# Later pacing of 32 small scatters, and their read-back moved behind the fifth expert's weights

## The chip, the cores and the metric

The kernel runs on one core of a Trainium2 chip. The time is device microseconds (us) of one whole execution. Three timed executions of the kernel before took 656.32, 656.92 and 656.56 us; the median is 656.56 us.

## The reference, cut to what matters

The program has two layers over x of shape (2, 1024, 128). Layer 0 is causal attention times the SiLU of a mixture of experts. Layer 1 is a rotation memory (cumulative sums of x times cosine and sine of a phase, a norm, two matrices with GELU) times the SiLU of a second mixture of experts. The change touches only the second mixture:

```python
expert_inputs = einsum('GSEC,GSM->EGCM', dispatch, x)        # 8 experts, 8 groups, 64 slots
layer_w0 = einsum('EGCM,EMH->EGCH', expert_inputs, w0_kernel)
layer_w1 = einsum('EGCM,EMH->EGCH', expert_inputs, w1_kernel)
hidden = gelu(layer_w0, approximate=True) * layer_w1          # H = 688
expert_outputs = einsum('EGCH,EHM->EGCM', hidden, wo_kernel)
out = einsum('EGCM,GSEC->GSM', expert_outputs, combine)       # each token: two of the slots
```

Each of the 2048 tokens goes to two experts. `posn[:, a, n]` holds, for the 128 tokens of tile n, the slot of choice a. A slot's result has to come back to its token.

## The kernel before, in words

Every engine has one program, written out in order, and engines meet only at counting semaphores: `then_inc` raises one, `wait_ge(Z[name], n)` holds the engine until it is n. The sync engine (SP) issues nearly all plain loads, one after another. If one of them waits, all later ones of SP wait behind it. GpSimd (POOL) issues the scatters, also strictly in order.

The second mixture is a loop over 8 experts, numbered 0 to 7. For an expert, TensorE (PE) makes six pairs of products of 512 slots: gate (L1757; L1755 for the last piece, which is gate and up in one) and up (L1760). ScalarE (ACT) applies GELU to each gate product (L733), and VectorE (DVE) multiplies it with the up product (L1362). That multiplication is the "up product" of the title: it raises `hid1_done`, six times for each expert, 48 times in all. After the first two pieces of the next expert, PE does the down product (L1771, 48 matmuls) and raises `ew_free`; DVE copies the result out (L1369) and raises `y1_done`. Behind the last expert PE goes on with the two matrices of the rotation memory's branch (L1815, L1826). Between these multiplications DVE works through the rotation memory, at fixed places in the same loop, and ACT does its sine and absolute value after piece 1 of expert 2 and its cosine after piece 1 of expert 3. The distance from one L1771 to the next is one expert period.

PE may run two pieces ahead. A gate product waits for the GELU of two pieces before (`act1_done`), an up product for the multiplication of two pieces before (`hid1_done`).

The scatters of the change are made by `scatter_destinations` (L553). It writes, for each of the 2 x 16 tiles, 128 words of 4 bytes into the array `dest1` in device memory: at the slot's place, the row that the slot's result must go to. I number them 0 to 31 (16 a + n). SP reads `dest1` back as `dest` (L519) once all 32 have landed. Only then can POOL start the 32 result scatters (L585, four for each expert), which write each expert's output rows to device memory. They go through a buffer of four experts: DVE's copy for expert e waits, from e = 4 on, for the four result scatters of expert e - 4.

`load_expert(e)` on SP (L505 to L513) loads an expert's weights into the buffer that expert e - 2 has left. Its first three loads wait until PE has made the last gate product of expert e - 2, its last three wait for the down product of expert e - 2. In the kernel before, the order on SP is: expert 3's weights, the read-back (L519), expert 4's weights.

Of the kernel before, what the change touches and what calls it, by code (L numbers as in the profile page):

```python
# [18 lines left out]
NT = T // P  # L19
# [190 lines left out]
def build(nc, x, WQ, WK, WV, WO, gate, w1, w2, w3, WomT, b_om, log_scale, gamma, beta, W1T, b1, W2T, b2,  # L210
# [10 lines left out]
    with ExitStack() as ctx:  # L221
# [3 lines left out]
        def sem(name):  # L225
            return ctx.enter_context(nc.semaphore(name))
# [120 lines left out]
        Z = {n: sem(n) for n in names.split()}  # L347
# [34 lines left out]
        def _(sp):  # L382
# [118 lines left out]
            def load_expert(e):  # L501
                s = e % 2
                if e >= 2:
                    sp.wait_ge(Z["g1_ps"], HT * (e - 1))
                sp.dma_start(ew[s][0], w0k[e, :, :]).then_inc(w_in[s], 16)  # L505
                sp.dma_start(ew[s][1][:, TW:H1], w1k[e, :, 0:H1 - TW]).then_inc(w_in[s], 16)
                sp.dma_start(ew[s][1][:, 0:TW], w1k[e, :, H1 - TW:H1]).then_inc(w_in[s], 16)
                if e >= 2:
                    sp.wait_ge(Z["ew_free"], e - 1)
                sp.dma_start(ew[s][2][0:125, 0:4, :],  # L510
                             wok[e, 0:500, :].rearrange("(k p) m -> p k m", p=125)).then_inc(wo_in[s], 16)
                sp.dma_start(ew[s][2][0:124, 4, :], wok[e, 500:H1 - TW, :]).then_inc(wo_in[s], 16)
                sp.dma_start(ew[s][2][P - TW:P, 5, :], wok[e, H1 - TW:H1, :]).then_inc(wo_in[s], 16)  # L513

            for e in range(E):
                load_expert(e)
                if e == 3:
                    sp.wait_ge(Z["scattered"], 16 * 4 * NT)
                    sp.dma_start(dest, dest1[0:SLOTS1, :].rearrange("(p j) o -> p (j o)", p=P)).then_inc(Z["dest_in"], 16)  # L519
            for s in range(4):  # L520
# [11 lines left out]
        @block.gpsimd  # L532
        def _(pool):
            pool.memset(V, 1.0).then_inc(Z["v_ones"], 1)
            pool.memset(mpart[:, :, :], -BIG).then_inc(Z["mem_set"], 1)
            pool.memset(MP, 0.0).then_inc(Z["mem_set"], 1)

            def scatter_rows():

                for a in range(2):  # L540
                    for n in range(NT):
                        pool.wait_ge(Z["e_ready"], SCATTER_AT + SCATTER_EVERY * (NT * a + n))
                        pool.indirect_dma_start(xs0, bass.IndirectOffsetOnAxis(ap=posn[:, a, n:n + 1], axis=0),  # L543
                                                rows[a][:, n, :], None).then_inc(Z["scattered"], 16)

            def scatter_destinations():

                for a in range(2):
                    pool.wait_ge(Z["routed"], 2 + a)
                    for n in range(NT):  # L550
                        if NT * a + n >= 4:
                            pool.wait_ge(Z["hid1_done"], (2 * (NT * a + n) - 4) // 3)
                        pool.indirect_dma_start(dest1, bass.IndirectOffsetOnAxis(ap=posn[:, a, n:n + 1], axis=0),  # L553
                                                idt[:, NT * a + n:NT * a + n + 1], None).then_inc(Z["scattered"], 16)

            pool.wait_ge(Z["pads_in"], 16)
            pool.wait_ge(Z["routed"], 1)
            pool.wait_ge(Z["rows_ready"], 1)
            scatter_rows()

            def scatter_results(c, j):
                pool.wait_ge(Z["y_done"], j + 1)
                pool.nop(nofuse=True)
                pool.indirect_dma_start(ys[0], bass.IndirectOffsetOnAxis(ap=yb0[:, c, ID_META:ROW].bitcast(I32), axis=0),  # L564
                                        yb0[:, c, 0:D], None).then_inc(yb_out[c], 16)
            with pool.Fori(0, NB0 // YB0) as i:
                for c in range(YB0):
                    scatter_results(c, YB0 * i + c)
            for j in range(NB0 // YB0 * YB0, NB0):
                scatter_results(j % YB0, j)  # L570

            pool.wait_ge(Z["pads1_in"], 32)
            pool.wait_ge(Z["pv_done"], NG * NS)
            for s in range(2):
                pool.memset(ew[s][2][0:P - TW, 5, :], 0.0)
            pool.wait_ge(Z["disp_ps"], G1)
            for s in range(2):
                ins = pool.memset(hT1[0:P - TW, s, 5, :], 0.0)
            ins.then_inc(Z["tail_zero"], 1)
            scatter_destinations()  # L580
            pool.wait_ge(Z["dest_in"], 16)
            for e in range(E):
                pool.wait_ge(Z["y1_done"], e + 1)
                for m in range(4):
                    pool.indirect_dma_start(  # L585
                        ys[1], bass.IndirectOffsetOnAxis(ap=dest[:, 4 * e + m:4 * e + m + 1], axis=0),
                        yb1[:, e % 4, m, :], None).then_inc(y1_out[e % 4], 16)
# [3 lines left out]
        def _(act):  # L591
# [91 lines left out]
            for k in range(NG + 1):  # L683
                for step in PLANS[k]:
                    if step[0] == "exp":
                        _, stage, heads = step
                        half, kt = STAGES[stage]
                        r, n = NS * k + stage, 512 - max(0, P * kt - 512 * half)
                        act.wait_ge(Z["e_ready"], e + 1)
                        if r >= 4:  # L690
                            act.wait_ge(Z["pv_done"], r - 3)
                        act.activation(Pr[:, r % 4, heads[0]:heads[-1] + 1, 0:n],  # L692
                                       ring_e[e % 3][:, 0:len(heads) * n].rearrange("p (j c) -> p j c", j=len(heads)), ACT.Exp,
                                       scale=SCALE).then_inc(Z["e_free"], 1)
                        e += 1
                    elif step[0] == "counts":
                        act.wait_ge(Z["gates_d"], 1)
                        act.activation(rs[:, 3, :], rs[:, 2, :], ACT.Exp).then_inc(Z["gates_exp"], 1)
                    elif step[0] == "evac":
                        _, g, half = step  # L700
                        act.wait_ge(Z["pv_done"], NS * g + (NS if half else QT // 2))
                        if g >= 1:
                            act.wait_ge(Z["turned"], 2 * (g - 1) + half + 1)
                        act.copy(OT[:, 512 * half:512 * half + 512], O).then_inc(Z["o_evac"], 1)
                    elif step[0] == "experts0":
                        experts0()
                    elif step[0] == "gate":
                        gate_half(0, step[1])
                    elif step[0] == "scale":
                        act.wait_ge(Z["ld_vecs"], 16 * 5)  # L710
                        act.activation(vecs[:, 12:13], vecs[:, 1:2], ACT.Exp).then_inc(Z["el_done"], 1)
# [63 lines left out]
        def _(dve):  # L775
# [296 lines left out]
            for k in range(-1, NG + 1):  # L1072
                for step in PLANS[k]:
                    if step[0] == "p1":
                        _, g, heads, i, half = step
                        n = min(512, (i + 1) * P - 512 * half)
                        ps = unit_ready()
# [831 lines left out]
```

## Time and profile before

| what | value |
|---|---|
| median of the timed executions | 656.56 us |
| the profiled execution's own time | 658.66 us |
| its span | 656.9 us |
| PE busy / DVE busy / ACT busy / POOL busy | 91% / 75% / 50% / 25% |
| second mixture's experts | about 475 to 613 us of the span |
| packets of the software queue (POOL) | 4320, 3.2% of 16 DMA engines' time |

A timeline row gives start, busy time, engine, line and operation, and in square brackets how long the engine had been idle before it and whose work ended that idle time. "Remote" there means that the awaited semaphore rose just before the start, while no instruction ended at that moment that could have raised it. A row of a windows view gives a stretch, its length, and for each engine the busy time and the number of instructions in it, then the granted share of TensorE's full clock (1.00 is 2.4 GHz, 0.50 is 1.2 GHz), the share of DMA engine time, and GB/s.

### The profile page before, as it was taken

How to read it: one execution, taken by the hardware profiler on the slowest of the kernel's cores; microseconds unless marked ns; L12 is line 12 of the kernel's file. 1: busy time of each engine (PE TensorE's matmuls, PEld its weight loads, DVE VectorE, ACT ScalarE, POOL GpSimd, SP SyncE). 2: the span in 40 equal slices, each digit the busy share in tenths (PEclk: the TensorE clock that was granted, in tenths of full speed). 3: DMA queues.
4: the chain of work that ended last, by engine and by line, in shares of the span. 5: the costliest groups of instructions: out<-in, count | busy, mean ns of one | idle time of the engine just before them, and what ended most of it. 6: DMA issues, size and time to landing. Idle time of an engine off the chain costs nothing. (4 is left out here: it accounts for less than half of the span.)

```text
span 656.9 us, 12382 instructions
## 1 busy us (share of the span) xinstructions
PE 594.7 (91%) x4214; PEld 365.6 (56%) x4215; DVE 490.1 (75%) x1169; ACT 325.3 (50%) x581; POOL 163.5 (25%) x146
## 2 busy tenths in 40 slices
PE   1878999999999999899999998949989799999996
PEld 0523644444453545899999843426446355555654
DVE  7799889999988898455555598246898288987455
ACT  1752367575766766555555467721323352254134
POOL 2000000000143441133333300000068668843200
PEclk9877799999999999999999999987999899999999
DMA  8980606060713181211111070061012114320232
GB/s 191 239 281 22 219 16 185 19 201 3 204 38 100 36 224 25 49 49 45 48 48 40 25 197 2 2 197 61 1 44 66 22 47 120 109 81 17 69 76 64
DMA packets 53692, 57.18 MB, mean 87 GB/s; under 512 B 8651, under 2 KB 37355, under 8 KB 53595
## 3 DMA queue, kind: packets, MB, share of 16 engines
q1 hardware_dynamic: 49310, 49.73, 27.1%
q0 software_dynamic: 4320, 6.81, 3.2%
q8 instruction: 29, 0.48, 0.3%
q14 instruction: 21, 0.16, 0.1%
q10 hardware_dynamic: 12, 0.01, 0.0%
HBM read 42.19 MB, written 18.85 MB: 93 GB/s over the span
## 5 line engine op out<-in xcount | busy, mean ns | idle before, releaser
L692 ACT ACTIVATE arena<-banks 128x512 f32<-128x512 f32 (+1 forms) x304 | 156.2, 586 | 100.3 <-PE banks L1588 57.9
L1602 PE MATMUL banks<-arena 96*128 96x512 bf16 (+3 forms) x384 | 120.4, 343 | 5.2 <-DVE mpart L1082 2.8
L1585 PE MATMUL banks<-arena 128*128 128x512 bf16 (+3 forms) x384 | 116.8, 331 | 6.5 <-ACT arena L692 2.8
L1085 DVE TENSOR_REDUCE mpart<-banks 128x1 f32<-128x512 f32 x128 | 85.8, 684 | 9.0 <-PE banks L1602 8.4
L1082 DVE CUSTOM_DVE_ANT_0 banks<-banks,arena 128x512 f32<-128x512 f32 (+1 forms) x128 | 78.9, 636 | 9.6 <-PE banks L1602 6.6
L1523 PE MATMUL banks<-arena 128*128 128x128 f32 x624 | 76.3, 275 | 1.0 <-ACT arena L642 1.0
L1523 PEld LDWEIGHTS banks<-arena 128*128 128x128 f32 x624 | 72.8, 192 | 1.5 <-ACT arena L642 1.5
L1644 PE MATMUL banks<-arena 128*9 128x512 f32 (+3 forms) x768 | 70.8, 487 | 0.0
L733 ACT ACTIVATE arena<-banks 125x512 f32<-125x512 f32 (+2 forms) x48 | 28.5, 595 | 81.0 <-PE banks L1757 57.0
L1585 PEld LDWEIGHTS banks<-arena 128*128 128x128 bf16 x384 | 38.0, 100 | 53.9 <-issue 26.0
L543 POOL DMA_INDIRECT slots<-rows_a,posn x16 | 15.5, 967 | 194.6 <-PE banks L1585 185.0
L564 POOL DMA_INDIRECT results<-arena x39 | 37.8, 969 | 87.6 <-DVE arena L1016 87.6
L1602 PEld LDWEIGHTS banks<-arena 96*128 96x128 bf16 x384 | 38.2, 101 | 36.3 <-DVE mpart L1082 9.1
L585 POOL DMA_INDIRECT results<-arena x32 | 44.7, 1395 | 37.3 <-DVE arena L1369 24.6
L1006 DVE TENSOR_TENSOR arena<-banks,arena 128x512 f32<-128x512 f32 x39 | 27.0, 692 | 33.9 <-PE banks L1523 29.3
L1588 PE MATMUL banks<-bc 128*128 128x128 bf16 x256 | 49.8, 222 | 0.0
L553 POOL DMA_INDIRECT dest<-idt,posn x32 | 44.8, 1400 | 17.2 <-issue 8.8
L1771 PEld LDWEIGHTS banks<-arena 125*128 125x128 f32 (+2 forms) x384 | 44.1, 191 | 5.2 <-issue 5.2
L1757 PE MATMUL banks<-arena 128*125 128x512 f32 (+1 forms) x80 | 42.1, 608 | 4.9 <-issue 3.4
L1760 PE MATMUL banks<-arena 128*125 128x512 f32 (+1 forms) x80 | 42.7, 616 | 3.9 <-DVE arena L1362 3.4
L1362 DVE TENSOR_TENSOR arena<-banks,arena 125x512 f32<-125x512 f32 (+2 forms) x48 | 32.3, 690 | 18.3 <-PE banks L1760 10.1
L1771 PE MATMUL banks<-arena 125*128 125x128 f32 (+2 forms) x384 | 44.3, 275 | 1.0 <-issue 1.0
(289 smaller groups left out, 901.9 us busy)
## 6 DMA issues: line engine op xcount, KB each, us to landing
k_parts<-arena SPq DMA_DIRECT2D x6, 768.0 KB, 7.8
arena<-in_L_ffn_experts_w_dram SPq DMA_DIRECT2D x2, 2048.0 KB, 10.6
arena<-results SPq DMA_DIRECT2D x8, 512.0 KB, 6.8
arena<-k_parts SPq DMA_DIRECT2D x7, 576.0 KB
arena<-q_parts SPq DMA_DIRECT2D x28, 144.0 KB
arena<-in_L_ffn_w_kernel_dram SPq DMA_DIRECT2D x8, 344.0 KB
slots<-in_pad_rows_dram SPq DMA_DIRECT2D x1, 2535.0 KB, 11.0
arena<-slots SPq DMA_DIRECT2D x39, 65.0 KB
```

The costliest lines, as they stand in the source:

```text
L553: pool.indirect_dma_start(dest1, bass.IndirectOffsetOnAxis(ap=posn[:, a, n:n + 1], axis=0), idt[:, NT * a + n:NT * a + n + 1], None).then_ ...
L585: pool.indirect_dma_start(ys[1], bass.IndirectOffsetOnAxis(ap=dest[:, 4 * e + m:4 * e + m + 1], axis=0), yb1[:, e % 4, m, :], None).then_i ...
L692: act.activation(Pr[:, r % 4, heads[0]:heads[-1] + 1, 0:n], ring_e[e % 3][:, 0:len(heads) * n].rearrange("p (j c) -> p j c", j=len(heads)) ...
L1082: ins = dve.tensor_tensor_reduce(ps[:, 0:n], ps[:, 0:n], tail_mask[:, 512 - n:512], 1.0, -BIG, ALU.add, ALU.max, part)
L1085: ins = dve.tensor_reduce(part, ps[:, 0:n], AX_X, ALU.max)
L1523: ins = pe.matmul(psE[:, c % 2, 512 * w + P * k:512 * w + P * k + P], w_now[:, c % 2, w, P * k:P * k + P], xT0[:, c % 2, :], start=True, s ...
L1585: ins = pe.matmul(ring_e[e % 3][:, at * n:at * n + n], QK[:, slot, j, 1, P * kt:P * kt + P], QK[:, slot, j, 0, q:q + n], start=True, stop= ...
L1588: ins = pe.matmul(ring_e[e % 3][:, at * n:at * n + P], upper_b, ident_b, start=False, stop=True)
L1602: ins = pe.matmul(ps[:, at * n:at * n + n], QK[0:TALL, slot, j, 0, P * i:P * i + P], QK[0:TALL, slot, j, 1, 512 * half:512 * half + n], st ...
L1644: ins = pe.matmul(O[32 * j:32 * j + DK + 1, q:512], V[:, QT * b + kt, HG * hq + j, :], Pr[:, r % 4, j, 0:512 - q], start=(kt == 0), stop=( ...
L1760: pe.matmul(psE[0:hn, k % 2, 512:1024], ew[s][1][:, TW + h0:TW + h0 + hn], XT1[:, e, :, :], start=True, stop=True).then_inc(Z["u1_ps"], 1)
L1771: ins = pe.matmul(psM[:, e % 2, P * m:P * m + P], hT1[HD[k], s, k, P * m:P * m + P], ew[s][2][HD[k], k, :], start=(k == 0), stop=(k == HT ...
```

## The change

Before, scatters 0 to 3 wait for nothing but the routing result, and scatter k from 4 on waits until `hid1_done` is (2k - 4) // 3, so the last waits for 19 (the first piece of expert 3). Now every scatter waits, scatter k for 1 + 3k // 4, so the last waits for 24 (the last piece of expert 3). And the read-back stands on SP behind expert 4's weights, not ahead of them.

```diff
             for e in range(E):
                 load_expert(e)
-                if e == 3:
+                if e == 4:
                     sp.wait_ge(Z["scattered"], 16 * 4 * NT)
                     sp.dma_start(dest, dest1[0:SLOTS1, :].rearrange("(p j) o -> p (j o)", p=P)).then_inc(Z["dest_in"], 16)
...
                 for a in range(2):
                     pool.wait_ge(Z["routed"], 2 + a)
                     for n in range(NT):
-                        if NT * a + n >= 4:
-                            pool.wait_ge(Z["hid1_done"], (2 * (NT * a + n) - 4) // 3)
+                        pool.wait_ge(Z["hid1_done"], 1 + 3 * (NT * a + n) // 4)
                         pool.indirect_dma_start(dest1, bass.IndirectOffsetOnAxis(ap=posn[:, a, n:n + 1], axis=0),
                                                 idt[:, NT * a + n:NT * a + n + 1], None).then_inc(Z["scattered"], 16)
```

What stands on SP between the weights of expert 3 and those of expert 5 (a minus is a row of before alone, a plus one of the changed kernel alone):

```order
 L512 DMA arena<-in_L_ffn_wo_kernel_dram 124x128
 L513 DMA arena<-in_L_ffn_wo_kernel_dram 64x128
-L519 DMA arena<-dest 128x32 [waits scattered]
 L505 DMA arena<-in_L_ffn_w_kernel_dram 128x688 [waits g1_ps]
 L506 DMA arena<-in_L_ffn_w_kernel_dram 128x624
@@ -152,4 +151,5 @@
 L512 DMA arena<-in_L_ffn_wo_kernel_dram 124x128
 L513 DMA arena<-in_L_ffn_wo_kernel_dram 64x128
+L519 DMA arena<-dest 128x32 [waits scattered]
 L505 DMA arena<-in_L_ffn_w_kernel_dram 128x688 [waits g1_ps]
 L506 DMA arena<-in_L_ffn_w_kernel_dram 128x624
```

One load, with its wait, has moved past the six loads of one expert. On POOL, the scatters of the destinations before (L553), and the first result scatters behind them:

```order
L553 DMA dest<-idt,posn 8192x1 [waits routed]
L553 DMA dest<-idt,posn 8192x1 x3
L553 DMA dest<-idt,posn 8192x1 [waits hid1_done] x12
L553 DMA dest<-idt,posn 8192x1 [waits hid1_done,routed]
L553 DMA dest<-idt,posn 8192x1 [waits hid1_done] x15
L585 DMA results<-arena 8192x128 [waits y1_done,dest_in]
```

and now, where the same scatters are L552 and the results L584, since the file is one line shorter:

```order
L552 DMA dest<-idt,posn 8192x1 [waits hid1_done,routed]
L552 DMA dest<-idt,posn 8192x1 [waits hid1_done] x15
L552 DMA dest<-idt,posn 8192x1 [waits hid1_done,routed]
L552 DMA dest<-idt,posn 8192x1 [waits hid1_done] x15
L584 DMA results<-arena 8192x128 [waits y1_done,dest_in]
```

The number and order of POOL's instructions are the same; four of them have a wait that they had not, and all waits are for other counts. The programs of PE, DVE and ACT are unchanged.

## Rows read from the trace of the kernel before

**Rows 1.** Windows view: expert periods, from one L1771 to the next; columns as described above.
```profile
490.80:506.20 15.40, 15.05 (x71) 9.40 (x70) 13.88 (x14) 3.57 (x6) 12.96 (x9) 1.00 0.27 68
506.20:529.70 23.50, 18.61 (x71) 9.85 (x70) 9.79 (x12) 9.87 (x12) 16.19 (x15) 0.85 0.08 17
529.70:545.90 16.20, 15.12 (x72) 9.43 (x71) 14.28 (x13) 8.13 (x9) 10.45 (x7) 1.00 0.38 104
545.90:561.20 15.30, 15.09 (x72) 9.42 (x71) 13.01 (x11) 3.57 (x6) 12.56 (x10) 1.00 0.38 123
```

**Rows 2.** Timeline of PE, 506 to 620 us.
```profile
506.27 5.52 PE L1771 MATMUL banks<-arena 125*128 125x128 f32 x48
...
511.63 1.02 PE L1757 MATMUL banks<-arena 128*125 128x512 f32 x2
...
513.35 1.02 PE L1757 MATMUL banks<-arena 128*125 128x512 f32 x2
...
518.63 1.12 PE L1757 MATMUL banks<-arena 128*124 128x512 f32 x2 [3.41 <-issue]
...
542.35 1.12 PE L1757 MATMUL banks<-arena 128*125 128x512 f32 x2 [1.08 <-DMA arena<-in_L_ffn_w_kernel_dram]
...
613.38 7.03 PE L1815 MATMUL banks<-arena 128*128 128x512 f32 x16
```

**Rows 3.** Timeline of all engines, 506 to 542 us: DVE, ACT and SP.
```profile
506.88 1.28 DVE L1362 TENSOR_TENSOR arena<-banks,arena 125x512 f32<-125x512 f32 x2
...
515.86 0.28 SPq L510 DMA_DIRECT2D arena<-in_L_ffn_wo_kernel_dram  x1
515.86 0.69 DVE L1369 COPY arena<-banks 128x512 f32<-128x512 f32 x1 [7.70 <-remote]
...
517.98 0.60 ACT L733 ACTIVATE arena<-banks 125x512 f32<-125x512 f32 x1 [5.45 <-remote]
...
522.40 1.34 ACT L733 ACTIVATE arena<-banks 125x512 f32<-125x512 f32 x2 [3.83 <-remote]
...
523.16 0.69 DVE L1362 TENSOR_TENSOR arena<-banks,arena 125x512 f32<-125x512 f32 x1 [3.01 <-PE banks L1760]
...
541.71 1.42 DVE L1362 TENSOR_TENSOR arena<-banks,arena 124x512 f32<-124x512 f32 x2
```

**Rows 4.** Timeline of POOL, 479 to 584 us.
```profile
479.22 0.97 POOL L553 DMA_INDIRECT dest<-idt,posn  x1 [4.68 <-DVE posn L1254]
...
505.94 0.96 POOL L553 DMA_INDIRECT dest<-idt,posn  x1 [0.30 <-issue]
...
518.57 0.96 POOL L553 DMA_INDIRECT dest<-idt,posn  x1 [0.30 <-issue]
520.43 0.96 POOL L553 DMA_INDIRECT dest<-idt,posn  x1 [0.91 <-issue]
524.13 2.75 POOL L553 DMA_INDIRECT dest<-idt,posn  x1 [2.75 <-DVE arena L1362]
...
534.42 2.09 POOL L553 DMA_INDIRECT dest<-idt,posn  x1 [0.30 <-issue]
540.73 1.78 POOL L585 DMA_INDIRECT results<-arena  x1 [4.22 <-DMA arena<-dest]
...
584.02 0.96 POOL L585 DMA_INDIRECT results<-arena  x1 [5.89 <-DVE arena L1369]
```

**Rows 5.** Timeline of SP, 486 to 538 us.
```profile
486.67 0.36 SPq L505 DMA_DIRECT2D arena<-in_L_ffn_w_kernel_dram  x1
...
502.42 0.35 SPq L505 DMA_DIRECT2D arena<-in_L_ffn_w_kernel_dram  x1
...
537.69 0.35 SPq L519 DMA_DIRECT2D arena<-dest  x1
538.08 0.43 SPq L505 DMA_DIRECT2D arena<-in_L_ffn_w_kernel_dram  x1
```

**Rows 6.** Windows view, one stretch of 2 us, same columns as Rows 1.
```profile
522.00:524.00 2.00, 0.98 (x2) 0.50 (x2) 0.84 (x2) 1.19 (x2) 0.00 (x0) 0.50 0.03 4
```

## The prediction, made before the changed kernel was run

> **What bounds the kernel now.** I read the page first: PE is busy 91% of the span. Behind the experts its matrices (L1815) start with no wait in front [rows 2], so what the experts save reaches the end. Time is to be had only where PE stands still or is slowed. Then I cut the windows view at the down products, one row for each expert period, and that view decides the case. Three of the four periods shown take 15.3 to 16.2 us; the one from expert 1's down product to expert 2's takes 23.50 [rows 1]. PE did the same work in it (71 instructions, as in its neighbour), but DVE was busy only 9.79 us of it, and the granted clock was 0.85 in the mean, in one stretch of it 0.50, that is 1.2 GHz [rows 1, 6].
>
> The timelines of that period show what happened. PE's down product began at 506.27 and ended 5.52 us later, at 511.79 [rows 2]. Two programs wait for just that: DVE's copy (L1369) and SP's load (L510). Both started at 515.86, so the semaphore was seen some 4.1 us after the work that raises it. PE's next gate product began at 511.63 and ended by 512.65; ACT's GELU of it started at 517.98, 5.3 us late, and ends an idle time that the trace calls remote. ACT's next one, at 522.40, belongs to the gate product that PE began at 513.35, so it was some 8 us late [rows 2, 3]. PE itself then had nothing to do: its next gate product waits for the GELU of two pieces before, and came at 518.63, after 3.41 us with no product at all [rows 2]. After 523.16 everything runs on time again. I call this the hold. It is no lack of an engine: the news of finished PE work came late.
>
> **What the hold goes with.** The scatters. POOL issued 32 of them from 479.22 to 534.42. Twelve stand between 505.94 and 520.43, the last gap aside one every 1.26 us (0.96 busy and 0.30 between), with no wait that held them, because POOL was behind its pacing: at 506.88 DVE made up products 13 and 14, and those allow scatters up to number 24 at once [rows 3, 4]. The first late signal (511.79) comes 5.9 us into this burst, the worst near its end. Then scatter 26 had to wait for up product 16, which itself came late, at 523.16, and in this pause the late signals all arrived [rows 3, 4]. DMA engines were no bottleneck: over the whole period their share is 0.08 [rows 1]. My reading is that a dense run of these 128-word scatters to device memory backs up a path on which PE's signals travel too. The trace shows the coincidence, not the path.
>
> **Term 1, the pacing.** Scatter k now waits for up product 1 + 3k // 4. Up products 13 and 14 of the trace ended by 508.16 [rows 3]; they now release scatters 16 to 18, where before they released all to 24. So the burst ends with 18, at about 510.2 (scatters 16, 17 and 18 at 507.7, 508.9 and 510.2 with 1.26 us each). Scatter 19 waits for up product 15. Without the hold, gate and up of piece 2 end by 513.5 (gate begun at 511.63, the next gate at 513.35 [rows 2]), and DVE's 0.69 us behind them ends by about 514.3. That is a pause of 4 us on POOL just where the hold began. And the pacing now regulates itself: a late up product stops the scatters at once, where before POOL had ten in hand.
>
> What is the period worth without the hold? Its PE work is that of its neighbours. Those took 15.40 and 15.30, and 16.20 with a weight wait of 1.08 inside, so 15.12 [rows 1, 2]. ACT has sine and absolute value here, but is through with them by 512.53 (5.45 before 517.98 [rows 3]), when the gate product it needs has only just ended. I take 15.6, a little above the neighbours, for the two long ACT instructions. Saved: 23.5 - 15.6 = 7.9 us. The low clock falls inside the hold (PE had stood still before it) and goes with it; it is in the 7.9 and not added.
>
> Bounds of this term. Best case: the period sinks to 15.1, 8.4 saved. Worst of this reading: scatters still come in pairs and threes and leave some of the hold. The neighbour 490.8 to 506.2 had scatters in it (9 POOL instructions) and took 15.40 [rows 1], so that density costs next to nothing; I leave 0.5 us for it, and keep 0 to 8 as its bounds.
>
> **Term 2, the read-back on SP.** Before, SP stood at L519 until scatter 31 (issued 534.42) had landed, and went on at 537.69; only then could expert 4's weights be issued, at 538.08, though their buffer had been free since expert 2's last gate product. PE waited 1.08 us for them before 542.35 [rows 2, 5]. Now they are issued when that gate product is done, which without the hold is about 518, 4.3 us or so before they are in (538.08 to 542.35), against a need at about 533. The wait of 1.08 goes. What is late next there is the DVE chain of the period (14.28 busy of 16.20 [rows 1]), so I credit 0.8 and keep 0 to 1.1.
>
> What the move costs: the read-back now stands behind six loads, the last three of which wait for expert 2's down product, about 527 without the hold. Scatter 31 waits for up product 24. Before that was the second of the pair at 541.71, ended 543.1 [rows 3]; minus 7.9 and 0.8 it is 534.5. The scatter starts there and, as before, 3.3 us pass to the read-back (534.42 to 537.69), so L519 is issued at about 538 and the result scatters start at about 541, as before (540.73 [rows 4]). Expert 5's weights, queued behind it, come at 538.4 and are needed at about 547 (expert 4's were at 541, minus 8.7, plus a period of 15.3). DVE's copy for expert 4 (its down product begins at 561.20 [rows 1] and takes 5.5, minus 8.7: 558) needs the first four result scatters, landed by about 549: 9 us to spare. POOL has caught up with the experts before 584.02, where it waited 5.89 us for DVE [rows 4]; 9 us earlier experts leave it just in time. So the move costs nothing; this cover fails only if the read-back comes over 9 us later.
>
> The four scatters that had no wait start at 481 instead of 479.22; nobody waits for them. 32 waits on POOL are met by an engine that is 25% busy.
>
> **Sum.** 7.9 - 0.5 + 0.8 = 8.2 us. The profiled execution took 658.66 us, 2.1 above the median of the three timed ones and with a span of 656.9. The timed ones lie within 0.6 us of each other, so the hold is hardly a rare accident: I take it off the median too, 656.56 - 8.2 = 648.4.
>
> **A rule that speaks against it.** The rows show ACT idle 5.45 us behind a finished PE product while POOL's scatters run [rows 3, 4]. The Trainium skill's page "SBUF — State Buffer", section "Who interferes with whom", says that DMA never contends with a compute engine and that "PE and ACT never wait on anyone". By that rule the scatters could not be what holds PE and ACT. The trace has no case that decides it: the rule is about ports of the on-chip memory, and what came late here is a signal. The rival that follows is worked out from the rows.
>
> **Rivals.**
> (a) The hold has another cause and stays. For it: PE, ACT and DVE share nothing with POOL in the program at that point, and scatters 14 to 18 may still come 1.3 us apart. Against it: it starts in the burst and ends in POOL's pause. Then term 1 is 0, and term 2 alone is left, 0.8 to 1.1 us: about 655.6. The later pacing costs nothing even then: up product 24 ends at 542, the read-back at about 545.5 is still in time.
> (b) The hold shrinks but stays: POOL keeps three or four scatters in hand at 504 to 510, and half of the delay remains. 656.6 - 4 - 0.8 = 652.
> (c) Slower: the hold comes from scatters beside weight loads, and now there are two. Before it, expert 3's weights were issued at 502.42 among scatters [rows 5]. Now expert 4's weights go out near 518 to 526 among scatters 22 to 26, which before they could not, since SP stood at L519 until the scatters had landed. If both periods have a hold of 7.9 us, the time is 656.6 + 7.9 - 1 = 663.5. It decides from the point where expert 3's period exceeds 17 us. Against it: expert 2's weights, issued at 486.67 amid scatters [rows 5], brought no hold.
>
> **Chances.** Forecast, hold gone or nearly: 0.47 (647 to 650). (b): 0.16. (a): 0.20. (c), with smaller second holds that end just above the old time: 0.17. A change under 0.2%, 1.3 us, can't be told from none: faster 0.63, same 0.20, slower 0.17. The range reaches from 647.0 over (b) and (a) to 658.5, and leaves out the bulk of (c); the forecast's own is 647 to 650.
>
> **What would show it.** Right: the period between the down products of experts 1 and 2 at 15.3 to 16, DVE's copy L1368 within 0.2 us of the down product's end, no clock below 1.00 from 475 to 610, no wait of PE for weights at expert 4, POOL in pauses of 2 us and more around 511 to 514, result scatters from about 541. Wrong: a period over 18 us anywhere; then look whether scatters or weight loads surround it. Wrong in term 2: a DVE copy that waits for result scatters.

## The result and the profile after

The changed kernel took 650.28 us (median of 7 executions, 649.79 to 654.0), against a median of 656.92 for the kernel before, measured beside it. The ratio of the two is estimated as 0.9906, with a 95% interval of 0.9879 to 0.9933: 6.2 us faster, 4.4 to 7.9 (the two medians lie 6.6 apart). Forecast were 8.2 us and 648.4.

The profiled execution has a span of 648.0 us against 656.9, 8.9 less. Not all of this is the change: PE's first down product of the experts begins at 489.11 instead of 490.86, so 1.75 us were already won where nothing was changed. Other runs below spread as much there. What the change did stands in the expert periods. The windows view after, cut at the down products (columns as in [rows 1]):

```profile
489.10:504.50 15.40, 15.05 (x71) 9.39 (x70) 13.89 (x15) 3.60 (x7) 12.96 (x9) 1.00 0.26 69
504.50:521.70 17.20, 15.36 (x72) 9.32 (x71) 9.45 (x12) 9.78 (x11) 11.48 (x11) 1.00 0.25 44
521.70:537.10 15.40, 15.07 (x72) 9.39 (x71) 13.73 (x12) 8.08 (x9) 12.77 (x9) 1.00 0.16 46
537.10:552.40 15.30, 15.09 (x72) 9.43 (x71) 13.67 (x12) 3.57 (x6) 9.90 (x8) 1.00 0.44 138
```

The long period went from 23.50 to 17.20, that is 6.3 us, and its clock from 0.85 to 1.00. The next went from 16.20 to 15.40, 0.8 us: PE's wait for expert 4's weights is gone. Together 7.1 us. But 17.20 is not the 15.4 of its neighbours. PE's timeline after (start, busy, idle before it in brackets) shows what is left:

```profile
504.52 5.52 PE L1770 MATMUL banks<-arena 125*128 125x128 f32 x48
514.76 1.12 PE L1756 MATMUL banks<-arena 128*124 128x512 f32 x2 [1.29 <-ACT arena L732]
```

And those of DVE and ACT:

```profile
514.07 0.69 DVE L1368 COPY arena<-banks 128x512 f32<-128x512 f32 x1 [7.66 <-remote]
...
514.12 1.08 ACT L732 ACTIVATE arena<-banks 125x512 f32<-125x512 f32 x2 [3.33 <-PE banks L1756]
```

The down product ended at 510.04, and DVE saw it at 514.07: 4.0 us late, as in [rows 3], where it was 4.1. What is new is that the lateness ends there. At 514.07 to 514.12 DVE and ACT are both released, and ACT makes two GELUs in a row. Before, the later signals were later still [rows 3]. POOL's timeline after:

```profile
480.11 2.80 POOL L552 DMA_INDIRECT dest<-idt,posn  x1 [7.31 <-DVE arena L1361]
...
510.51 0.96 POOL L552 DMA_INDIRECT dest<-idt,posn  x1 [0.30 <-issue]
511.77 0.96 POOL L552 DMA_INDIRECT dest<-idt,posn  x1 [0.30 <-issue]
515.71 0.96 POOL L552 DMA_INDIRECT dest<-idt,posn  x1 [2.98 <-DVE arena L1361]
...
538.47 0.96 POOL L552 DMA_INDIRECT dest<-idt,posn  x1 [0.30 <-DVE arena L1361]
543.00 1.08 POOL L584 DMA_INDIRECT results<-arena  x1 [3.57 <-DMA arena<-dest]
...
591.31 0.96 POOL L584 DMA_INDIRECT results<-arena  x1 [5.83 <-DVE arena L1368]
```

The pause of some 3 us is there, but it comes late. Scatter 18, the last of the dense run (scatters that follow each other every 1.26 us), started at 511.77, 7.25 us after the down product began. I had it at 510.2 with the down product at 506.27, that is 3.9 us after it. So the pause, 512.73 to 515.71, begins when the hold is already 2.7 us old, and ends it. Against [rows 4] the dense run ends seven scatters earlier, with 18 and not 25. The pause is as long as it is because scatter 19 waits for up product 15, which itself came late. SP issues expert 4's weights at 517.63, not 538.08 [rows 5], and the read-back behind them:

```profile
517.63 0.35 SPq L505 DMA_DIRECT2D arena<-in_L_ffn_w_kernel_dram  x1
...
540.61 0.35 SPq L519 DMA_DIRECT2D arena<-dest  x1
541.01 0.43 SPq L505 DMA_DIRECT2D arena<-in_L_ffn_w_kernel_dram  x1
```

### The profile page after: what moved, and what is told of

Its sections match the earlier page's. It is cut to its first block and busy times, and to the rows that moved or that the text cites. A ratio compares the mean times of both kernels' runs of the same rounds, so it can differ in the third digit from the quotient of the medians.

```text
span 648.0 us, 12383 instructions
## 1 busy us (share of the span) xinstructions
PE 591.2 (91%) x4214; PEld 365.1 (56%) x4215; DVE 489.7 (76%) x1169; ACT 325.2 (50%) x581; POOL 165.7 (26%) x146
## 5 line engine op out<-in xcount | busy, mean ns | idle before, releaser
L552 POOL DMA_INDIRECT dest<-idt,posn x32 | 47.0, 1469 | 19.6 <-DVE arena L1361 12.3
L584 POOL DMA_INDIRECT results<-arena x32 | 44.7, 1396 | 25.6 <-DVE arena L1368 13.2
L1759 PE MATMUL banks<-arena 128*125 128x512 f32 (+1 forms) x80 | 41.8, 603 | 4.3 <-DVE arena L1361 4.3
L1756 PE MATMUL banks<-arena 128*125 128x512 f32 (+1 forms) x80 | 41.1, 596 | 1.7 <-ACT arena L732 1.3
L1534 PE MATMUL banks<-arena 128*128 x312 | 41.3, 275 | 0.7 <-DVE arena L1015 0.7
```

The lines of the kernel that those rows point to most:

```text
L1756: pe.matmul(psE[0:hn, k % 2, 0:512], ew[s][0][:, h0:h0 + hn], XT1[:, e, :, :], start=True, stop=True).then_inc(Z["g1_ps"], 1)
L1759: pe.matmul(psE[0:hn, k % 2, 512:1024], ew[s][1][:, TW + h0:TW + h0 + hn], XT1[:, e, :, :], start=True, stop=True).then_inc(Z["u1_ps"], 1)
```

## The experiments

Every run is compared with the kernel before on its own chip. Four kernels ran on one chip, the next four on a second, the last four on a third. "Period" is the one from expert 1's down product to expert 2's unless another is named.

**1. The pacing alone.** The changed kernel with the read-back where it was:

```diff
-                if e == 4:
+                if e == 3:
```

> The new pacing alone; the read-back stays ahead of expert 4's weights. In the changed kernel scatter 31 was issued at 538.47 and the read-back at 540.61; SP would then issue expert 4's weights only at about 541, they are in 4.3 us later (538.08 to 542.35 before), at 545.3, and PE wants them at about 532. Theory (the gain is the pacing's, but it needs the move): the period of expert 1 to 2 stays at 17.2 as in the changed kernel, and PE waits some 13 us for weights at expert 4, so 650.3 + 13 = 663 us, slower than before. Rival (the two parts are independent, the move is worth the 1.08 us wait that it removed): 651.4 us.

Measured: 665.41 us, ratio 1.0146 (1.0121 to 1.017), slower, as the theory had it (663; its rival 651.4). The period is 17.20 as in the changed kernel, and then comes, on PE and on SP:

```profile
546.60 2.07 PE L1756 MATMUL banks<-arena 128*125 128x512 f32 x2 [11.96 <-DMA arena<-in_L_ffn_w_kernel_dram]
```
```profile
542.07 0.35 SPq L519 DMA_DIRECT2D arena<-dest  x1
542.46 0.43 SPq L505 DMA_DIRECT2D arena<-in_L_ffn_w_kernel_dram  x1
```

The two parts aren't independent. The later pacing needs the read-back moved; without it expert 4's weights would wait for scatters that now end later.

**2. The read-back alone.** The changed kernel with the old pacing.

> The read-back behind expert 4's weights, with the old pacing. Theory: the hold stays whole (period of expert 1 to 2 at 23.5 us), PE's wait of 1.08 us for expert 4's weights goes: 656.9 - 0.8 to 1.1 = 656.0 us. Rival (the hold of before comes from weight loads beside scatters, so earlier weights for expert 4 make a second one): a period over 17 us also at expert 2 to 3, and over 658 us.

Measured: 656.14 us, ratio 1.000 (0.9976 to 1.0024). The windows view, three periods:

```profile
489.10:504.50 15.40, 15.05 (x72) 9.38 (x71) 13.88 (x15) 3.64 (x7) 12.96 (x9) 1.00 0.27 67
504.50:527.10 22.60, 17.41 (x72) 9.60 (x71) 9.54 (x12) 9.86 (x11) 15.96 (x15) 0.92 0.19 49
527.10:542.50 15.40, 15.07 (x72) 9.40 (x71) 13.73 (x12) 8.07 (x9) 8.36 (x6) 1.00 0.26 75
```

The hold stays, at 22.60. One execution of each kernel was profiled, so nothing is to be read from the 0.9 between this and the 23.50 of before. The period behind it is 15.40: no second hold, though expert 4's weights now go out among scatters (they were issued from 521.97 on). My slower rival (c) falls with this.

**3. No scatter at the end of the down product.** The changed kernel, with scatters from 16 on held until up product 15:

```diff
-                        pool.wait_ge(Z["hid1_done"], 1 + 3 * (NT * a + n) // 4)
+                        k = NT * a + n
+                        pool.wait_ge(Z["hid1_done"], 1 + 3 * k // 4 if k < 16 else max(15, 1 + 3 * k // 4))
```

> The changed kernel, and scatters 16 to 31 wait for up product 15 at least, so that scatter 15 is the last before PE's down product of expert 1 ends. Theory (PE's signals come late until about 0.6 us after the last packet of a dense run of scatters has been read): in the changed kernel scatter 18's packets end at 513.51 and PE's signals were seen at 514.07; here scatter 15's packets end at about 509.7, so the signal at 510.0 is at most 0.4 us late, the period of expert 1 to 2 is 15.4 to 15.8 instead of 17.2, and the time about 648.8 us. Rival (the first 4 us of lateness, 4.05 in the kernel before and 4.01 in the changed one, are of another cause, such as ACT's table loads or sine at that place): the period stays 17.2, the time 650.3 us.

Measured: 650.01 us, ratio 0.9901 (0.9881 to 0.9921). The down product ended at 511.67, and DVE's copy followed at once. Its row, and the windows view:

```profile
511.71 0.69 DVE L1369 COPY arena<-banks 128x512 f32<-128x512 f32 x1 [3.66 <-PE banks L1771]
```

```profile
506.20:521.60 15.40, 15.07 (x72) 9.40 (x71) 9.54 (x11) 9.86 (x11) 9.22 (x8) 1.00 0.24 70
521.60:537.00 15.40, 15.07 (x72) 9.40 (x71) 13.73 (x12) 8.05 (x9) 12.96 (x9) 1.00 0.12 24
537.00:556.20 19.20, 16.61 (x72) 10.01 (x71) 16.88 (x14) 3.58 (x6) 13.14 (x9) 0.91 0.33 98
```

The hold is gone altogether, with all the rest of the program in place: sine, absolute value, table loads, down product. But 3.9 us (19.20 against 15.30) came back two periods later. The scatters end later, the read-back with them, and expert 5's weights stand behind it; PE waited 2.60 us for them and ran at half clock for a while after. The profiled execution (653.16) was 3.1 us above the median, so in most executions this wait was probably smaller.

**4. One scatter in flight.** The old pacing, late read-back, and scatters 13 to 20 each wait for all earlier ones to land:

```diff
+                        if 13 <= NT * a + n <= 20:
+                            pool.wait_ge(Z["scattered"], 32 * NT + 16 * (NT * a + n))
```

> The old pacing with the read-back behind expert 4's weights, and scatters 13 to 20 each wait until all earlier ones have landed, so that they come some 3.2 us apart from about 504 on, right through the place of the hold. Theory (density makes the lateness): signals of PE are late by under 1 us, the period of expert 1 to 2 is 15.4 to 16.4, the time 648.5 to 650. Rival (any scatter there holds PE's signals, or the place does): the first 4 us remain, 17.2 to 23.5 for the period, 650 to 656.

Measured: 668.89 us, ratio 1.0185 (1.0162 to 1.0208). The total is a miss, the mechanism a hit. The first three periods are all 15.4: no hold. POOL's timeline shows the spacing, PE's what it cost:

```profile
509.01 0.95 POOL L555 DMA_INDIRECT dest<-idt,posn  x1 [3.74 <-DMA dest<-idt,posn]
512.26 0.95 POOL L555 DMA_INDIRECT dest<-idt,posn  x1 [2.29 <-DMA dest<-idt,posn]
515.13 0.96 POOL L555 DMA_INDIRECT dest<-idt,posn  x1 [1.92 <-DMA dest<-idt,posn]
```
```profile
568.70 2.07 PE L1759 MATMUL banks<-arena 128*125 128x512 f32 x2 [18.49 <-DMA arena<-in_L_ffn_w_kernel_dram]
```

Scatters passed through the place of the hold, 3 us apart, and held nothing. But the last was issued at 561.52, and expert 5's weights waited for it.

**5 to 7. The stop, with the read-back behind expert 5's weights.** All have `if e == 5:` on SP. Run 5 stops at scatter 16 as run 3 did, run 7 at 18 (`k < 18`), run 6 has the old waits throughout, but for scatters from 16 on never a count below 15.

> Scatters 16 to 31 wait for up product 15 at least, as in the run that stopped at 16, and the read-back now stands behind expert 5's weights, so that these need not wait for it. In the run that stopped at 16 there was no hold, but PE stood 2.60 us for expert 5's weights, and after it at 1.2 GHz for a while: its period of expert 3 to 4 was 19.2 instead of 15.3. Theory: no hold and no such wait, 650.0 less 3.9 = 646.3 us if the result scatters, which start at 549, still come in time for DVE's copy of expert 4's result; if they don't, up to 2 us are lost there, so 646.3 to 648.5. Rival (read-back and result scatters become the limit): 650 or more.

> As the run before it in this list, but scatters 0 to 15 with the old waits (the first four with none), and 16 to 31 with the old waits or up product 15, whichever is later. Theory: scatters start 1.9 us earlier and POOL, which is behind its pacing there anyway, has one more done when it stops; no hold; the read-back comes up to 2 us earlier and the time is the same as in that run or up to 1 us less, 646 to 648. Rival: the later pacing from 16 on also matters (a second dense run at the down product of expert 2): a period above 17 us there and 648 to 650.

> As the first run in this list, but POOL stops only at scatter 18, so two more stand in the dense run: 16 and 17, the last packets some 2.5 us later, at about 2.2 us past the end of expert 1's down product. Theory (a signal of PE is late until about 0.6 us after the last packet of the dense run): lateness 2.8 us, the period of expert 1 to 2 about 16.0 to 16.4 and the time 0.6 to 1 us above the first run. Rival (once the run is dense enough a signal is late by a fixed 4.0 us, as in all four kernels that had a hold): 4.0 us, 17.2 and 1.8 us above.

Measured: run 5 652.67 us, ratio 0.9903 (0.9877 to 0.9929); run 6 650.49, 0.9891 (0.9852 to 0.993); run 7 649.97, 0.9866 (0.984 to 0.9893). None has a hold: the period is 15.39 or 15.40 in all three. Runs 5 and 6 missed the times that I expected of them (646.3 to 648.5 and 646 to 648). In run 5 the expert period that begins at 552.87 took 19.60 instead of 15.8, and DVE's timeline says why:

```profile
564.19 0.69 DVE L1369 COPY arena<-banks 128x512 f32<-128x512 f32 x1 [2.96 <-DMA results<-arena]
```

It is the copy for expert 4, which must wait for expert 0's result scatters: the read-back at 550.48 was too late for them. Behind it PE stood 2.85 us and then ran at half clock. Run 6, with the read-back at 547.43, lost 2.88 us on PE at the same place. In run 7 it was issued at 544.53 and nobody waited. For run 7 neither number of its expectation came. Its down product ended at 511.58, and there was no lateness at all, which run 10 takes up:

```profile
511.62 0.69 DVE L1369 COPY arena<-banks 128x512 f32<-128x512 f32 x1 [3.66 <-PE banks L1771]
```

**8 and 11. Fewer rows in a scatter.** The old pacing, late read-back; scatters 13 to 31 write only 32 rows (run 8) or 64 (run 11), the other destinations being left out, so that these two kernels don't compute the whole result.

> The old pacing, read-back behind expert 4's weights, as in the run with the read-back alone (656.1 us, period of expert 1 to 2 at 22.6), but scatters 13 to 31 write only the first 32 of their 128 rows; the other destinations are left out, so their results go to rows that nobody reads. Theory (it is the number of small writes in flight that counts, a quarter here): no hold, period 15.4 to 15.8, about 649 us. Rival (the number of scatter instructions or of their semaphore increments counts): the hold stays, 20 to 23 us, 654 to 656 us.

> The old pacing with the read-back behind expert 4's weights; scatters 13 to 31 write 64 of their 128 rows, the other destinations are left out. With 128 rows the hold was 7 us (period 22.6), with 32 it was gone. Theory (small writes in flight count): half the writes at the same pace of instructions are drained in time, period under 16, about 649. Rival (a scatter instruction with its increments counts, and 32 rows are a special case): 17 to 23 us, 651 to 656.

Measured: 32 rows 648.83 us, ratio 0.9847 (0.9814 to 0.988), period 15.40, no hold. 64 rows 659.37 us, ratio 1.0033 (1.0009 to 1.0056), the longest hold of all. DVE's and POOL's timeline of it:

```profile
520.56 0.69 DVE L1370 COPY arena<-banks 128x512 f32<-128x512 f32 x1 [13.37 <-remote]
```
```profile
515.76 0.90 POOL L554 DMA_INDIRECT dest<-idt,posn  x1 [0.30 <-issue]
516.96 0.90 POOL L554 DMA_INDIRECT dest<-idt,posn  x1 [0.30 <-issue]
522.20 0.90 POOL L554 DMA_INDIRECT dest<-idt,posn  x1 [4.34 <-DVE arena L1363]
```

The down product had ended at 510.81; its signal came 9.8 us late, and only when the dense run was over. Half the writes, with one scatter every 1.20 us instead of 1.26, did not shorten it. So the count of written words alone doesn't explain the hold. Run 8 (every 1.17 us, the last dense one 4.6 us past the down product) contradicts the count of instructions just as much. It ran on a chip where I profiled no kernel with a hold, but the kernel before took 658.57 us there, 9.7 more than run 8, so it very probably had its hold there too. What of a scatter counts stays open.

**9, 10 and 12. Changed kernel, stop at 18, stop at 23, on one chip.** Run 9 is the changed kernel, run 10 is run 7, run 12 has the old waits up to scatter 22 (`k < 23`) and `if e == 5:`; its scatter 23 then waits for up product 18.

> The changed kernel itself, once more, beside the three runs below on the same chip. So far the kernels with a hold were profiled on other chips than the run that stopped at 18. Theory (the hold belongs to the kernel): ew_free of expert 1's down product is seen 4.0 us late, that period is 17.2 us, and the time is 0.990 of the kernel before. Rival (it depends on the chip): no hold, and the time is that of the run that stops at 18.

> The run that stopped at 18 with the read-back behind expert 5's weights, once more, on the same chip as the changed kernel. Its dense run of scatters is one shorter than the changed kernel's: the last begins 6.0 us after the start of expert 1's down product, there 7.25. Theory (one scatter makes the difference): no hold, 1.8 us less than the changed kernel, so 0.987 of the kernel before. Rival (the chip made the difference): hold of 4 us and the changed kernel's time.

> The old pacing up to scatter 22, then up product 15 at least; read-back behind expert 5's weights. The last scatter of the dense run begins about 9.8 us after the start of expert 1's down product (7.25 in the changed kernel, 6.0 in the run that stopped at 18, no stop in the kernel before). Theory (the hold lasts as long as the dense run): the period is between the 17.2 of the changed kernel and the 22.6 of the read-back alone, about 19 to 20 us, the time about 652. Rival (past a threshold the hold is a fixed 4 us): 17.2 us, 650.

Measured: run 9 651.92 us, ratio 0.9901 (0.9875 to 0.9927); run 10 649.90, 0.987 (0.9836 to 0.9903); run 12 654.10, 0.9938 (0.9913 to 0.9963). Run 10's DVE and POOL timelines:

```profile
514.89 0.69 DVE L1369 COPY arena<-banks 128x512 f32<-128x512 f32 x1 [6.39 <-remote]
```
```profile
511.34 0.96 POOL L553 DMA_INDIRECT dest<-idt,posn  x1 [0.30 <-issue]
512.61 0.96 POOL L553 DMA_INDIRECT dest<-idt,posn  x1 [0.30 <-issue]
516.53 0.96 POOL L553 DMA_INDIRECT dest<-idt,posn  x1 [2.97 <-DVE arena L1362]
```

The down product ended at 512.12, so the signal was 2.8 us late, what I had expected of run 7, and neither the 0 nor the 4 us of run 10's own expectation. In run 7 the same program had none, on another chip. There is one profiled execution of each, and the two ratios (0.9866 and 0.987) don't tell them apart, so chip or execution, something outside the program has a part in whether the hold begins. Its length, once it has begun, goes with the dense run: run 12's period is 20.4, where its rival of a fixed 4 us asked for 17.2. The profiled runs in a table, ordered by where the last scatter of the dense run starts, counted from the end of the down product. Run 4 has no dense run; run 8 stands apart because of its 32 rows:

| run | last dense scatter | first signal late by | period |
|---|---|---|---|
| 6, stop at 16, old waits before | -4.6 | 0 | 15.4 |
| 3 and 5, stop at 16 | -2.1 | 0 | 15.4 |
| 7, stop at 18, second chip | +0.5 | 0 | 15.4 |
| 10, stop at 18, third chip | +0.5 | 2.8 | 15.9 |
| changed kernel | +1.7 | 4.0 | 17.2 |
| 1, changed pacing, old read-back | +1.7 | 4.1 | 17.2 |
| 9, changed kernel, third chip | +1.7 | 4.2 | 17.4 |
| 12, stop at 23 | +4.3 | 4.2 | 20.4 |
| 11, 64 rows | +6.2 | 9.8 | 24.3 |
| 2, old pacing | +8.6 | 4.1 | 22.6 |
| before | +8.6 | 4.1 | 23.5 |
| 8, 32 rows | +4.6 | 0 | 15.4 |

With the old 128 rows, the longer the run, the longer the period. In runs 9, 10 and the changed kernel the late signals all arrive within 1.3 to 1.6 us of the end of the last dense scatter's record (511.77 + 0.96 to 514.07; 512.61 + 0.96 to 514.89). In the longer runs some come in between, about 4 us late, and the rest only at the end.

## Why the prediction was right, and where its sizes were off

**The hold and its cause.** Right, and now shown rather than argued: taking scatters away from the place (run 3), or spacing them (run 4), removes the hold with all else left in place; run 2 shows that the pacing and not the move of the read-back is what shortens it. Rival (a), another cause, is refuted by runs 3 and 4. Not shown is the path that I supposed, on which scatters and PE's signals meet.

**Between the forecast and rival (b).** The forecast was a hold gone or nearly. What came was a hold that shrank, because POOL had scatters in hand, which is rival (b)'s mechanism: of the 8.1 us by which the period stood above 15.4, 1.8 remained, where (b) had left half. The time lies halfway between the forecast's 648.4 and (b)'s 652. Of the two reasons that I gave for the pacing, the pause placed "just where the hold began" failed, since the hold began first. The other one worked: a late up product stops the scatters at once. That it was enough to leave only 1.8 us is in part luck.

**Term 1, the pacing: forecast 7.4 us net (7.9 less 0.5), measured 6.3.** The step that failed is "scatters 16, 17 and 18 at 507.7, 508.9 and 510.2". I took the wait for the only thing that holds a scatter. But POOL was still behind its pacing: its first scatter started at 480.11 and took 2.80 us, many of the next 1.7 us and more, and scatter 16 started only at 509.25, seventeen scatters in 29 us. So the last scatter of the dense run began 1.7 us past the end of the down product, where the prediction had it 1.6 us before the end, and the period was 17.2 where 15.6 and the 0.5 that I left for a rest make 16.1. I had noted that the first signal comes late 5.9 us into the burst, and did not apply it: in the changed kernel the dense run began with scatter 12 at 504.20, 5.8 us before the signal that was late. Run 10 prices one scatter less at 1.5 us of the period (17.37 to 15.91).

**Term 2, the read-back: forecast 0.8, measured 0.8 in the period (16.2 to 15.4).** By itself it could not be told from no change (ratio 1.000). That the move costs nothing held: the read-back came at 540.61 (forecast 538), the result scatters at 543.00 (541), and no copy of DVE waited. The 2.6 us are the same mistake once more: scatter 31 started at 538.47, not at 534.5, because POOL was again behind its pacing (DVE had made up product 24 by 535.1). What I missed is its true worth. It is not the 1.08 us wait that it removed, but the 12 us wait that the new pacing would have made without it (run 1, 665.41 us against 650.28). I priced the edits one by one and not together.

**The cover of 9 us** for a late read-back was right, in part by luck. The prediction had the read-back at 538 and expert 4's down product at 552.5, so the cover ended with a read-back 5.5 us before that down product. In runs 5 and 6 it came 2.4 us before (550.48 against 552.87, 547.43 against 549.81), and DVE's copy waited 2.96 and 2.99 us, so the bound was at 5.4; in run 7 it came 7.6 before and nobody waited, in the changed kernel 11.8. Two sizes in it were off and cancel: the four result scatters let the copy go 13.7 us after the read-back, not 11 (run 5, 550.48 to 564.19), but DVE itself was free for the copy only 8.4 us after the down product's start, not 5.5.

**The other marks.** No clock below 1.00 in the periods: right. Expert 4 without a weight wait: right. A pause of POOL around 511 to 514: there, at 512.7 to 515.7. Period of 15.3 to 16 and DVE's copy within 0.2 us of the down product: wrong, 17.2 and 4.0.

**The rule that spoke against it.** The Trainium skill, page "SBUF — State Buffer", section "Who interferes with whom", has it that "PE and ACT never wait on anyone". In run 2 ACT stood 4.75 us before the GELU of the gate product behind the down product, in run 3, with the scatters moved, 0.15 us, and in run 4, with them spaced, 0.16 us. So ACT did wait on a signal of PE whose lateness goes with POOL's scatters. That is no contradiction of a rule about memory ports, but the rule is no ground for excluding a delay of signals.

**A version that looks better than both.** Stop at 18 with the read-back behind expert 5's weights: on one chip 649.90 us against 651.92 for the changed kernel and 657.87 for the one before, ratios 0.987 and 0.9901; on another chip 0.9866. The intervals overlap, and so do the single executions, just (648.77 to 650.79 against 650.39 to 652.59), but the profiles show the gain: a period of 15.4 to 15.9 instead of 17.2 to 17.4, and nothing given back.

## What to carry to other kernels

When several engines resume late at the same moment behind work that is long done, look at what POOL issued just before, and count its scatters by the time between them, not by their waits: an engine behind its pacing sends in one dense run whatever its waits allow. A wait that is moved later must be followed to the last thing queued behind it on every engine. Here each improvement of the pacing came back as a weight load or a buffer that waited, until the read-back was moved too, and past a certain point the move itself cost what it saved.

## What the runs showed of the hardware that I had not expected

In the runs of the table with a hold, a dense run of small scatters (one every 1.20 to 1.26 us, 64 or 128 rows of 4 bytes each) delayed the first signal of TensorE by 2.8 to 9.8 us. The DMA engines meanwhile were busy 2% of the time or less in the changed kernel from 510 to 514 us, and in run 11 from 510 to 520 us:

```profile
510.00:512.00 2.00, 2.00 (x6) 0.82 (x5) 0.00 (x0) 0.78 (x1) 1.39 (x3) 1.00 0.01 0
512.00:514.00 2.00, 1.48 (x4) 0.37 (x2) 0.00 (x0) 0.00 (x0) 0.74 (x1) 1.00 0.02 1
```

Signals of ScalarE were not seen late in such a stretch: in the kernel before, with the dense run still on, ACT's GELU of 517.98 took 0.60 us, and PE's next gate product, which waits for it, started at 518.63, 0.05 us behind its end [rows 2, 3]. Whether the signals or TensorE's true ends of work are late can't be told from these records, since its ends are modelled. The same program had 0 and 2.8 us in the profiled executions of runs 7 and 10, on two chips. Scatters of the same kind 3 us apart delayed nothing (run 4), nor did scatters of 32 rows every 1.17 us (run 8).
